# Row maxima of attention scores: one reduction across two PSUM banks instead of one per bank

## The reference

```
x = x + tanh(g_xattn) * attention(layernorm(x), ctx, ctx, mask)      # 16 heads of 16, 154 keys
x = x + tanh(g_ffn)   * ffn(layernorm(x))                            # 8 experts, top 2, sigmoid gates
attention: score = q k^T / 4;  softmax over the 154 keys;  out = attn v;  out Wo^T + bo
```

## Time and profile before

| what | value |
|---|---|
| median of 3 runs | 545.34 us (544.57 to 546.86) |
| the profiled execution | 547.0 us |
| its span, first to last instruction | 545.2 us |
| setup, about | 0 to 66.5 us |
| frames, about | 66.5 to 262 us |
| routing, then experts | 262 to 292 us, then to the end |
| maximum products L948 / reductions L648 | 128 of each, mean 340 ns / 474 ns |

### The profile page before, as it was taken

How to read it: one execution, slowest core, us unless ns; L and a number is a source line. 1 busy time by engine, 2 the same in 40 slices (tenths; PEclk the granted TensorE clock), 3 DMA queues, 4 the chain that set the end, 5 groups by cost and what they waited for, 6 DMA issues and landing times.

```text
span 545.2 us, 10979 instructions
## 1 busy us (share of the span) xinstructions
PE 433.0 (79%) x4070; PEld 335.5 (62%) x4070; DVE 326.9 (60%) x793; ACT 213.3 (39%) x538; POOL 159.9 (29%) x155
## 2 busy tenths in 40 slices
PE   3546739888888878884246999999999999999980
PEld 2432314545455534542246999999999999999970
DVE  7538587787887876664780455555455455455440
ACT  0220424564555554660000544444444444444420
POOL 8320010210112102110102145445445445445331
PEclk9957558999999997996555899999999999999995
DMA  7513022453435434330000122322322322323311
GB/s 220 166 35 107 18 94 84 143 151 92 146 106 154 111 90 144 117 131 30 10 0 19 41 40 40 56 46 40 49 51 40 56 45 41 54 45 41 41 21 19
DMA packets 33257, 40.03 MB, mean 73 GB/s; under 512 B 8607, under 2 KB 27859, under 8 KB 33203
## 3 DMA queue, kind: packets, MB, share of 16 engines
q0 software_dynamic: 12480, 27.25, 22.1%
q1 hardware_dynamic: 18081, 11.31, 7.3%
q10 hardware_dynamic: 2644, 0.77, 0.7%
HBM read 25.71 MB, written 9.44 MB: 64 GB/s over the span
## 4 chain that ended last, share of the span: by engine, by line
PE 63%; DVE 20%; DMA 6%; issue 4%; ACT 3%; ACTq 2%; SPq 0%; POOL 0%; DVEq 0%; POOLq 0%
PE bank L1162 7%; PE bank L1146 6%; PE bank L1148 6%; PE bank L1147 6%; PE bank L1163 6%; PE bank L1164 6%; PE bank L931 4%; DVE rowmax L648 4%; PE bank L1078 3%; PE bank L948 3%; PE bank L969 3%; DMA W_stage<-in_L_ffn_W 3%; PE bank L1100 3%; DVE W L666 3%; DVE stats L595 2%
## 5 line engine op out<-in xcount | busy, mean ns | idle before, releaser
L1146 PE MATMUL bank<-xh,W 128*128 128x128 f16 x624 | 121.7, 221 | 0.9 <-DVE xl L849 0.9
L1147 PE MATMUL bank<-xl,W 128*128 128x128 f16 x624 | 121.6, 221 | 0.0
L1148 PE MATMUL bank<-xh,W 128*128 128x128 f16 x624 | 121.6, 221 | 0.0
L558 ACT ACTIVATE h<-bank,b1T 128x128 f32<-128x128 f32 x312 | 89.1, 369 | 70.3 <-PE bank L1148 68.7
L399 POOL DMA_INDIRECT out_rows<-y_sb,scatter_tab x39 | 63.9, 1638 | 114.9 <-DVE y_sb L863 108.8
L1162 PE MATMUL bank<-W,hh 128*128 x312 | 85.4, 274 | 0.0
L1163 PE MATMUL bank<-W,hh 128*128 x312 | 85.0, 273 | 0.0
L1164 PE MATMUL bank<-W,hl 128*128 x312 | 85.0, 273 | 0.0
L855 DVE CAST hh<-h 128x512 f16<-128x512 f32 x78 | 33.9, 434 | 81.5 <-ACT h L558 81.5
L348 POOL DMA_DIRECT2D W_stage<-in_L_ffn_W x32 | 21.1, 658 | 176.6 <-DVE W L666 176.6
L648 DVE TENSOR_REDUCE rowmax<-bank 128x2 f32<-128x308 f32 x128 | 57.0, 474 | 23.8 <-PE bank L948 21.1
(11 more groups left out here) (177 smaller groups left out, 664.0 us busy)
## 6 DMA issues: line engine op xcount, KB each, us to landing
W_stage<-in_L_ffn_W POOLq DMA_DIRECT2D x32, 512.0 KB, 4.3
xn_scratch<-attn SPq DMA_DIRECT2D x8, 256.0 KB, 2.2
qst<-qh SPq DMA_DIRECT2D x56, 32.0 KB, 2.5
X_late<-in_x SPq DMA_DIRECT2D x6, 256.0 KB, 7.9
out_rows<-X_late SPq DMA_DIRECT2D x6, 256.0 KB, 2.5
qst<-ql SPq DMA_DIRECT2D x28, 32.0 KB, 3.2
xg<-xn_scratch,gather_tab POOLq DMA_INDIRECT x39, 3.4
out_rows<-y_sb,scatter_tab POOLq DMA_INDIRECT x39, 3.9
```

The lines of the kernel that those rows point to most:

```text
L558: ins = nc.scalar.activation(h32[s % 4][:, m * P:(m + 1) * P], H_BANKS[s % 4][:, m * P:(m + 1) * P], ACT.Gelu_apprx_tanh, scale=1.0 / W_SC ...
L1146: nc.tensor.matmul(dst, wh, xh[t % 3][:, cut], start=(c == 0), stop=False)
L1147: nc.tensor.matmul(dst, wh, xl[t % 3][:, cut], start=False, stop=False)
L1148: ins = nc.tensor.matmul(dst, wl, xh[t % 3][:, cut], start=False, stop=(c == KC - 1))
```

## The change

The two banks become one PSUM tensor `S1_BOTH` (two banks side by side), of which `S1_BANKS` are views. A max item is now a pair of products: `max_scores(v, m)` makes products 2m and 2m + 1 back to back, one in each bank, and signals once. `reduce_maxima(v, m)` takes the four maxima of both banks with one reduction of 2 x 2 x 154 = 616 elements. A pair waits for the reduction of the pair before. In the frames both products of a step stand ahead of `softmax_v`. The number of products stays 128; the number of reductions falls to 64.

```diff
-        bank = [... for i in range(8)]
+        bank = [... for i in range(6)]
+        S1_BOTH = es.enter_context(nc.psum_tensor("s1_both", [P, 2, 512], F32))
+        bank += [S1_BOTH[:, i, :] for i in range(2)]
...
-            return [(u + 1, NPAIR + 2 * i + k) for k in range(2)] if i < 4 else [(u + 2, 2 * (i - 6) + k) for k in range(2)] if i >= 6 else []
+            return [(u + 1, NPAIR // 2 + i)] if i < 4 else [(u + 2, i - 6)] if i >= 6 else []
...
-            def reduce_maxima(v, n):
-                g = 2 * NPAIR * v + n
+            def reduce_maxima(v, m):
+                g = NPAIR * v + m
                 dve.wait_ge(s1_filled, g + 1)
-                nc.vector.reduce_max(rowmax[:, 2 * n:2 * n + 2],
-                                     S1_BANKS[g % 2][:, 0:2 * S].rearrange("p (a s) -> p a s", a=2),
+                nc.vector.reduce_max(rowmax[:, 4 * m:4 * m + 4].rearrange("p (n a) -> p n a", n=2),
+                                     S1_BOTH[:, :, 0:2 * S].rearrange("p n (a s) -> p n a s", a=2),
                                      AX_X).then_inc(rowmax_done, 1)
...
-                if g >= 2:
-                    pe.wait_ge(rowmax_done, g - 1)
-                nc.tensor.matmul(S1_BANKS[g % 2][...], ...).then_inc(s1_filled, 1)
+                if g >= 1:
+                    pe.wait_ge(rowmax_done, g)
+                for n in (2 * m, 2 * m + 1):
+                    j, p = divmod(n, NPAIR)
+                    ins = nc.tensor.matmul(S1_BANKS[n % 2][...], ...)
+                ins.then_inc(s1_filled, 1)
...
-                    for v, n in maxima[0:1]:
+                    for v, n in maxima:
                         max_scores(v, n)
                     if i >= 1 and live(u):
                         softmax_v(ITEMS * u + i - 1)
-                    for v, n in maxima[1:2]:
-                        max_scores(v, n)
```

More of the change, by code:

```diff
@@ L172, in build @@
         y_sb = [sb(f"y_sb{i}", [P, D]) for i in range(3)]
-        bank = [es.enter_context(nc.psum_tensor(f"bank{i}", [P, 512], F32)) for i in range(8)]
+        bank = [es.enter_context(nc.psum_tensor(f"bank{i}", [P, 512], F32)) for i in range(6)]
+        S1_BOTH = es.enter_context(nc.psum_tensor("s1_both", [P, 2, 512], F32))
+        bank += [S1_BOTH[:, i, :] for i in range(2)]
         XT_BANKS, Y_BANKS, H_BANKS = bank[4:6], bank[6:8], bank[0:4]
@@ L643, in query_low @@
                 ins.then_inc(q_free, 1)
-            def reduce_maxima(v, n):
-                g = 2 * NPAIR * v + n
+            def reduce_maxima(v, m):
+                g = NPAIR * v + m
                 dve.wait_ge(s1_filled, g + 1)
-                nc.vector.reduce_max(rowmax[:, 2 * n:2 * n + 2],
-                                     S1_BANKS[g % 2][:, 0:2 * S].rearrange("p (a s) -> p a s", a=2),
+                nc.vector.reduce_max(rowmax[:, 4 * m:4 * m + 4].rearrange("p (n a) -> p n a", n=2),
+                                     S1_BOTH[:, :, 0:2 * S].rearrange("p n (a s) -> p n a s", a=2),
                                      AX_X).then_inc(rowmax_done, 1)
             def negate_maxima(v):
-                dve.wait_ge(rowmax_done, 2 * NPAIR * (v + 1))
+                dve.wait_ge(rowmax_done, NPAIR * (v + 1))
                 if v >= 1:
@@ L727, in _ @@
             weights_low(1)
-            for n in range(2 * NPAIR):
+            for n in range(NPAIR):
                 reduce_maxima(0, n)
@@ L731, in _ @@
             layernorm1(2)
-            for n in range(NPAIR):
+            for n in range(NPAIR // 2):
                 reduce_maxima(1, n)
@@ L932, in softmax_v, with max_scores @@
                 ins.then_inc(pv_done, 1)
-            def max_scores(v, n):
+            def max_scores(v, m):
                 b = v // UNITS_PER_BATCH
-                g = 2 * NPAIR * v + n
-                j, p = divmod(n, NPAIR)
-                if n == 0:
+                g = NPAIR * v + m
+                if m == 0:
                     pe.wait_ge(qst_landed[v % 3], QST_PER_USE * (v // 3 + 1))
@@ L945, in max_scores @@
                         pe.wait_ge(kv_made, 2 * KC)
-                if g >= 2:
-                    pe.wait_ge(rowmax_done, g - 1)
-                nc.tensor.matmul(S1_BANKS[g % 2][:, 0:2 * S].rearrange("p (a s) -> p a s", a=2), qst[v % 3][0:ROW_MAX, p, j * P:(j + 1) * P],
-                                 kst[0:ROW_MAX, b, p, :, 0:S], start=True, stop=True).then_inc(s1_filled, 1)
+                if g >= 1:
+                    pe.wait_ge(rowmax_done, g)
+                for n in (2 * m, 2 * m + 1):
+                    j, p = divmod(n, NPAIR)
+                    ins = nc.tensor.matmul(S1_BANKS[n % 2][:, 0:2 * S].rearrange("p (a s) -> p a s", a=2), qst[v % 3][0:ROW_MAX, p, j * P:(j + 1) * P],
+                                           kst[0:ROW_MAX, b, p, :, 0:S], start=True, stop=True)
+                ins.then_inc(s1_filled, 1)
             def turn_values(j, dst):
```

## The result

The changed kernel takes 551.31 us (median of 9 runs, 549.25 to 554.43), the one before 545.78 in the same sessions (9 runs, 544.57 to 547.70). The ratio is 1.0106, 95% interval 1.0077 to 1.0135: slower by 5.8 us by the ratio, 5.5 between the medians, with 3.8 forecast. The profiled execution has a span of 551.7 us against 545.2; it took 553.54 us, so it is one of the slower of the nine.

What follows compares the result with a forecast made beforehand. Setup bound by its reduction runs, frames by a PE-DVE dialogue. Setup +5.8, steps 0 to 3 -1.5, +0.2, -1.6, steps 6 to 9 +1.0, -0.1: sum +3.8 us, 549.1 us against the 545.34 median; range 544.6 to 553.2.

Steps and rivals of the forecast that it cites:

- The setup runs: Reductions of units 0 and 1 before the frames: pairs lose overlap, 1.58 us a cycle; +3.9 and +1.9, together +5.8 us.
- The wide reduction: DVE's 616-element reduction takes 0.79 us, saving 0.07 us where two reductions stood back to back.
- Frame 0: Steps 0 to 3 of frame 0: the statistics start 1.0 us earlier, a gain of 1.5 us.
- Odd frames: Steps 0 to 3 of frames 1, 3 and 5: +0.1 us in frame 3, +0.2 us for all.
- steps 6 to 9: Late steps of a frame: +0.33 us in each of frames 0, 2, 4; -0.1 us for frames 1, 3, 5.
- Even frames: Steps 0 to 3 of frames 2, 4 and 6: -0.6 us in frame 4, -0.4 in frame 6, -1.6 for all.
- its own sign: Wrong if setup runs keep near 8 and 4 us, or setup-end-to-routing changes by over 2 us from -2.0.
- The clock: PE's granted clock: lower, chance 0.09, 553.7 us; or 2.4 GHz in the setup runs, chance 0.06, 545.9 us.
- rival 2: PE waits longer, so its clock falls more often: two more falls, +4.6 us, 553.7 us; chance 0.09.
- Rival 1: Frames 1 to 6 all get step 3's gain, waits of steps 1 and 7 cost nothing: 546.0 us; chance 0.15.
- rival 3: A reduction over two banks costs as much as two, 0.95 us: +7.3 us, 552.6 us; chance 0.08.

Runs made afterwards that it cites:

- single products ahead: Against the kernel before: in the frames both products of a step stand ahead of the values product, each with its own handshake and reduction; 542.79 us, ratio 0.9945.
- filled waits in the setup: Changed kernel plus throwaway products on PE in the setup runs, 24 behind the first pair and 3 behind each other; 553.38 us, ratio 1.0152 to the kernel before.

## Why the prediction was right, and where its size was off

**The setup runs** were right: 11.9 and 5.6 us against 11.85 and 5.53. Pairs in the setup alone bring the 5.9 us, pairs in the frames alone bring no loss, and a second pair of banks removes it with the same reductions: it is the lost overlap. The 1.58 us cycle was 1.59, the reduction 0.797 us where 0.79 was taken by slope (the slope of the two rows, not rounded down, gives 0.80).

**The wide reduction** was right: 0.06 us a pair by the two cycles, 1.59 and 1.65.

**Frame 0** was right: 1.5 us back, the statistics 1.1 us earlier.

**Odd frames** came out at 0.2 for frames 3 and 5 where I had 0.1, and their steps 6 to 9 gave 0.2 in frames 1 and 3 where I had 0.07. In frame 1 I was wrong by using frame 3 for it: frame 1 has nothing to turn or to route between the pairs of step 0 and 1, PE arrives sooner and waits 0.68 us more where frame 3 waits 0.23. With pairs in the frames only, at full clock, this cost 0.8 instead of 0.4 with the steps 6 to 9 ahead of it.

**Even frames** were right: from the low query to the negation before to after, frame 4 took 9.24 us instead of 9.69, and frame 2 8.99 instead of 9.51; that is 0.5 each where I had 0.6. It is not the same in every profile: with pairs in the frames only frame 4 took 9.65. The wait for the query product in steps 6 to 9 cost 0.4 a frame, 0.33 forecast.

**By its own sign** the forecast failed for the frames: it called itself wrong if they change by more than 2 us from the -2.0 of the table. From the low query of unit 2 to the first operation of the routing they changed by +1.3 us, 3.3 away; 2.9 of that are the two falls of the clock. That the total still came near is right in mechanism for the setup and partly luck for the rest: without the two falls the profiles differ by 3.6 us, against 3.8, but in this 0.3 too much in frame 1 is set against 0.6 less in the routing, the experts and the start, on which nothing was forecast.

**The clock** is the term that was mis-sized. I put rival 2 at 0.09 and its like at zero in the sum. The profile of the changed kernel shows one fall more, in frame 1, worth 1.5 us (10.4 against 8.8 us from low query to negation), and an earlier one in the tail, 1.4. Which falls the other executions had is not recorded; their mean clocks say that five of nine had more than the other four. With 1.5 to 2.9 the sum of 3.8 becomes 5.3 to 6.7, and measured are 5.5 between the medians. The median of the four executions with the higher clock is 549.9 us, 0.8 over the forecast. That the change itself brings more falls is not shown: frame 1 fell in the kernel with single products ahead as well and held in two kernels with pairs in the frames, and the largest loss in the tail is that of the kernel with pairs in the setup only. What sets a fall off stays open. Rival 1 fell with the experiment on the frames alone as far as the second half of it goes (the waits of steps 1 and 7 do cost), rival 3 with the reduction of 797 ns.

The rule of the Trainium skill that I set beside rival 2 ("TensorE: Matmul & The Clock Gate", the second failure mode: idle times of PE between groups that cycle through PSUM banks make its clock swing) fits the rows of frames 1, 3 and 5 shown above, with PE waiting 1.30 to 1.37 and 0.2 to 0.7 us for a bank pair, but not the two profiles whose frame 1 has the same waits at 1.00; I had weighed it too low since the kernel before showed it only in frame 5. The other rule ("Advanced Engine Details and Errata", TRN2 Errata, one instruction over several banks) is true here for 0.06 us a pair, and in the setup runs it pays only with a second pair of banks.

## What to carry to other kernels

Before merging two operations that read alternate buffers, ask what fills the buffers meanwhile. The merged one needs a second merged buffer, or the cycle becomes the sum of both engines' times: here 1.59 us against 1.02, and 0.79 once two idle banks were lent to it. And take a change apart: its reordering of the products was worth 3 us in the frames, which the handshake that came with it hid.

## What was not expected of the hardware

Two waits of PE, of 1.30 to 1.37 and 0.2 to 0.7 us, went ahead of a fall to 1.2 GHz in frame 1 of the changed kernel's profile and of the one with filled waits in the setup, frame 3 of another and frame 5 of a third. The same waits in the other odd frames of these profiles did not, nor did they in frame 1 of two further profiles, while one wait of 0.98 us went ahead of such a fall in another. Each fall cost 1.5 to 3.4 us. The medians of the two groups of the changed kernel lie 3.6 us apart (549.9 and 553.5).
